# The smaller key by VectorE, the larger by GpSimd: sharing a bitonic sort's compare and exchange

## The reference, cut to what matters

```python
src = jnp.concatenate([edge_index[0], loops])      # 524288 edges, 50176 nodes
dst = jnp.concatenate([edge_index[1], loops])
e = jax.nn.leaky_relu(a_src[src] + a_dst[dst], negative_slope=0.2)
e_max = jax.ops.segment_max(e, dst, num_segments=M)
ee = jnp.exp(e - e_max[dst])
denom = jax.ops.segment_sum(ee, dst, num_segments=M)
```

## Time and profile before

| what | value |
|---|---|
| median of 3 runs | 11034.17 us (11019.4 to 11040.31) |
| the profiled execution's own time | 11027.03 us |
| its span in the trace | 11025.2 us |
| VectorE busy | 5592.9 us, 51% of the span |
| GpSimd busy | 6152.7 us, 56% |
| TensorE busy (products) | 4769.1 us, 43% |
| ScalarE busy | 3867.4 us, 35% |

### The profile page before, as it was taken

How to read it: one execution, slowest core, us unless ns; L and a number is a source line. 1 busy time by engine, 2 the same in 40 slices (tenths; PEclk the granted TensorE clock), 3 DMA queues, 4 the chain that set the end, 5 groups by cost and what they waited for, 6 DMA issues and landing times. The chain is left out here.

```text
span 11025.2 us, 125122 instructions
## 1 busy us (share of the span) xinstructions
PE 4769.1 (43%) x29069; PEld 2965.3 (27%) x29069; DVE 5592.9 (51%) x14901; ACT 3867.4 (35%) x9265; POOL 6152.7 (56%) x6259
## 2 busy tenths in 40 slices
PE   0111777777775998784232232232222323323000
PEld 0111666666663554552011011011111101101000
DVE  9997988888886776552121121211211212112477
ACT  0011777777772555332121121121111212212255
POOL 0000444444441221676777777777777777777675
PEclk9755999998996999887666666666666666666555
DMA  0000111111112222553222222222222222222366
GB/s 21 0 0 36 36 32 35 35 32 35 32 35 78 62 61 59 142 147 74 44 47 49 40 51 45 41 51 43 45 48 45 47 44 45 50 40 48 137 237 240
DMA packets 1325844, 659.79 MB, mean 60 GB/s; under 512 B 1058255, under 2 KB 1239100, under 8 KB 1320764
## 3 DMA queue, kind: packets, MB, share of 16 engines
q1 hardware_dynamic: 1142396, 576.49, 19.2%
q0 software_dynamic: 183104, 80.22, 6.2%
HBM read 344.86 MB, written 313.71 MB: 60 GB/s over the span
## 5 line engine op out<-in xcount | busy, mean ns | idle before, releaser
L1843 POOL DMA_INDIRECT gr_rec<-rec,gr_idx x4096 | 3963.3, 968 | 1248.8 <-issue 1247.9
L1864 PE MATMUL gr_p_h<-gr_tT,gr_w 128*128 128x512 f32 x1568 | 848.0, 695 | 3682.3 <-ACT gr_hT L1898 3648.9
L1983 DVE TENSOR_SCALAR gr_pen<-gr_same 128x64 f32<-128x64 f32 x64 | 13.7, 215 | 3170.5 <-DMA gr_rec<-rec,gr_idx 3170.5
L1864 PEld LDWEIGHTS gr_p_h<-gr_tT,gr_w 128*128 128x128 f32 x1568 | 347.0, 226 | 4164.8 <-ACT gr_hT L1898 3734.0
L549 POOL TENSOR_TENSOR at_sq<-at_qk 128x256 f32<-128x256 f32 x392 | 263.9, 673 | 2121.3 <-ACT at_qk L591 2118.9
L1911 ACT ACTIVATE gr_ee<-gr_dd 128x512 f32<-128x512 f32 x64 | 40.3, 629 | 3598.4 <-DVE gr_dd L2002 3598.4
L1869 PE MATMUL gr_p_y<-gr_hT,gr_w 128*128 128x512 f32 x1568 | 688.9, 592 | 0.0
L1963 DVE STREAM_TRANSPOSE gr_z<-gr_yb 128x2048 f32<-128x2048 f32 x98 | 226.5, 2311 | 895.4 <-ACT gr_yb L1903 863.9
L1898 ACT ACTIVATE gr_hT<-gr_p_h,gr_b 128x512 f32<-128x512 f32 x784 | 517.8, 688 | 190.2 <-PE gr_p_h L1864 186.9
L2151 POOL DMA_INDIRECT cb_a<-scan,cb_idx x392 | 503.9, 1286 | 133.7 <-issue 121.1
L1347 POOL DMA_INDIRECT adst<-co_rec,co_idx x448 | 422.8, 944 | 202.5 <-issue 148.5
(11 more groups left out here) (364 smaller groups left out, 13262.2 us busy)
## 6 DMA issues: line engine op xcount, KB each, us to landing
y<-gr_z SPq DMA_DIRECT2D x392, 256.0 KB, 5.2
cb_y<-y SPq DMA_DIRECT2D x28, 3584.0 KB
gr_rec<-rec,gr_idx POOLq DMA_INDIRECT x4096, 2.4
scan<-gr_out SPq DMA_DIRECT2D x64, 768.0 KB, 3.5
at_xs<-in_x_win SPq DMA_DIRECT2D x56, 448.0 KB, 3.9
x<-at_x SPq DMA_DIRECT2D x56, 448.0 KB, 4.5
ff_x<-x SPq DMA_DIRECT2D x56, 448.0 KB, 3.3
x<-ff_x SPq DMA_DIRECT2D x784, 32.0 KB
```

The costliest lines, as they stand in the source:

```text
L1843: nc.gpsimd.indirect_dma_start(out=rec[s][:, j, :], out_offset=None, in_=rec_dram, in_offset=bass.IndirectOffsetOnAxis(ap=idx[s][:, j:j + ...
L1864: nc.tensor.matmul(p_h[m % 4][:, :], w1[:, P * m:P * (m + 1)], tT[b.k][:, :], start=True, stop=True).then_inc(S["hp"], 1)
```

## The change

In every stage the 2048 pairs of a partition are split: 1280 (five eighths) stay with VectorE alone, and for 768 (three eighths) the minimum is still VectorE's, while GpSimd makes the maximum. It reads both keys as integers and adds them (32 bits) into a new tile `so_both`; when VectorE's minimum is there, it subtracts it from the sum, and what is left is the larger key's bits. One stage then has three VectorE instructions (a minimum of 768 pairs, a minimum and a maximum of 1280 pairs) and two GpSimd instructions (a sum and a difference, 768 elements each).

`pairs` chooses the columns. Up to width 256 GpSimd's pairs are all in columns 2560 to 4095; above that they are the last three eighths of each group. Two successive stages of width 256 or less thus touch the two column ranges independently, and `near` marks the second of such a pair (145 of the 190 stages): there the sum and the first minimum wait only for the last stage's first minimum and last difference. In the other 45 stages both engines wait for all of the stage before. The counter `pooled` counts GpSimd's instructions, and the flips, the turns and the code behind the sort wait for it as well.

```diff
+        both = sb("so_both", [P, EP // 2], I32)
+        pooled = Steps(sem("so_pooled"))
+        OWN = 2560
+        def pairs(tile, d, mirror, pool):
+            if d <= 256:
+                cols = tile[:, OWN:EP] if pool else tile[:, 0:OWN]
+                view = cols.rearrange("p (g h s) -> p g h s", h=2, s=d)
+                return view[:, :, 0, :], view[:, :, 1, ::-1] if mirror and d > 1 else view[:, :, 1, :]
+            lo, hi = (5 * d // 8, d) if pool else (0, 5 * d // 8)
+            view = tile.rearrange("p (g h s) -> p g h s", h=2, s=d)
+            if mirror:
+                return view[:, :, 0, lo:hi], view[:, :, 1, d - 1 - lo:d - 1 - hi if hi < d else None:-1]
+            return view[:, :, 0, lo:hi], view[:, :, 1, lo:hi]
...
-                at.append((s, m, t, f))
+                at.append((s, m, t, f, l))
+                small = item[0] == "stage" and item[3] <= 256
+                near.append(small and last)
+                last = small
                 if item[0] == "stage":
-                    s += 2
+                    s += 3
+                    l += 2
...
+            @block.gpsimd
+            def _(pool):
+                for item, by, (s, m, t, f, l) in zip(plan, near, at):
...
+                    lo, hi = pairs(a[:, :].bitcast(I32), d, mirror, True)
+                    small, large = pairs(b[:, :].bitcast(I32), d, mirror, True)
...
+                    pool.wait_ge(stepped.sem, s - 2 if by else s)
+                    if l:
+                        pool.wait_ge(pooled.sem, l)
+                    if m:
+                        pool.wait_ge(moved.sem, m)
+                    pooled.done_by(nc.gpsimd.tensor_tensor(sums, lo, hi, ALU.add))
+                    pool.wait_ge(pooled.sem, l + 1)
+                    pool.wait_ge(stepped.sem, s + 1)
+                    pooled.done_by(nc.gpsimd.tensor_tensor(large, sums, small, ALU.subtract))
...
-                        v.wait_ge(done.sem, s)
+                        v.wait_ge(done.sem, s - 2 if by else s)
+                        if l:
+                            v.wait_ge(pooled.sem, l)
...
-                        done.done_by(nc.vector.tensor_tensor(bv[:, :, 0, :], av[:, :, 0, :], av[:, :, 1, r], ALU.min))
-                        done.done_by(nc.vector.tensor_tensor(bv[:, :, 1, r], av[:, :, 0, :], av[:, :, 1, r], ALU.max))
+                        lo, hi = pairs(a[:, :], d, mirror, True)
+                        small, _ = pairs(b[:, :], d, mirror, True)
+                        done.done_by(nc.vector.tensor_tensor(small, lo, hi, ALU.min))
+                        lo, hi = pairs(a[:, :], d, mirror, False)
+                        small, large = pairs(b[:, :], d, mirror, False)
+                        if by:
+                            v.wait_ge(done.sem, s)
+                        done.done_by(nc.vector.tensor_tensor(small, lo, hi, ALU.min))
+                        done.done_by(nc.vector.tensor_tensor(large, lo, hi, ALU.max))
```

More of the change, by code:

```diff
@@ L183, in sort_edges @@
         with nc.Block() as block:
-            at, s, m, t, f = [], 7, 0, 0, 0
+            at, s, m, t, f, l = [], 7, 0, 0, 0, 0
+            near, last = [], False
             for item in plan:
-                at.append((s, m, t, f))
+                at.append((s, m, t, f, l))
+                small = item[0] == "stage" and item[3] <= 256
+                near.append(small and last)
+                last = small
                 if item[0] == "stage":
-                    s += 2
+                    s += 3
+                    l += 2
                 elif item[0] == "flip":
@@ L212, in _ @@
                 act.wait_ge(loaded, 64)
-                for item, (s, m, t, f) in zip(plan, at):
+                for item, (s, m, t, f, l) in zip(plan, at):
                     if item[0] == "flip":
@@ L216, in _ @@
                         act.wait_ge(stepped.sem, s)
+                        act.wait_ge(pooled.sem, l)
                         for c in range(NCH):
@@ L235, in _ @@
                     pe.wait_ge(stepped.sem, s)
+                    pe.wait_ge(pooled.sem, l)
                     if m:
@@ L244, in _ @@
                         last.then_inc(turned.sem, 1)
+            @block.gpsimd
+            def _(pool):
+                for item, by, (s, m, t, f, l) in zip(plan, near, at):
+                    if item[0] != "stage":
+                        continue
+                    _, a, b, d, mirror = item
+                    lo, hi = pairs(a[:, :].bitcast(I32), d, mirror, True)
+                    small, large = pairs(b[:, :].bitcast(I32), d, mirror, True)
+                    n = lo.shape[1] * lo.shape[2]
+                    sums = both[:, 0:n].rearrange("p (g s) -> p g s", g=lo.shape[1])
+                    pool.wait_ge(stepped.sem, s - 2 if by else s)
[7 more added lines that the diff above has]
+                    pooled.done_by(nc.gpsimd.tensor_tensor(large, sums, small, ALU.subtract))
             @block.vector
@@ L264, in _ @@
                 done.done_by(nc.vector.tensor_scalar(ka[:, :], kb[:, :], sgn[:, 0:1], None, ALU.mult))
-                for n, (item, (s, m, t, f)) in enumerate(zip(plan, at)):
+                for n, (item, by, (s, m, t, f, l)) in enumerate(zip(plan, near, at)):
                     if n == 8:
@@ L272, in _ @@
                         _, a, b, d, mirror = item
-                        v.wait_ge(done.sem, s)
+                        v.wait_ge(done.sem, s - 2 if by else s)
+                        if l:
+                            v.wait_ge(pooled.sem, l)
                         if m:
                             v.wait_ge(moved.sem, m)
-                        av = a[:, :].rearrange("p (g h s) -> p g h s", h=2, s=d)
-                        bv = b[:, :].rearrange("p (g h s) -> p g h s", h=2, s=d)
-                        r = slice(None, None, -1) if mirror and d > 1 else slice(None)
-                        done.done_by(nc.vector.tensor_tensor(bv[:, :, 0, :], av[:, :, 0, :], av[:, :, 1, r], ALU.min))
-                        done.done_by(nc.vector.tensor_tensor(bv[:, :, 1, r], av[:, :, 0, :], av[:, :, 1, r], ALU.max))
+                        lo, hi = pairs(a[:, :], d, mirror, True)
[7 more added lines that the diff above has]
+                        done.done_by(nc.vector.tensor_tensor(large, lo, hi, ALU.max))
                     elif item[0] == "turn":
@@ L285, in _ @@
                             done.done_by(nc.vector.tensor_copy(b[:, 512 * c:512 * c + 512], banks[c][:, :]))
-                assert done.n == end
+                assert done.n == end and pooled.n == l + 2 * (item[0] == "stage")
                 v.wait_ge(done.sem, end)
+                v.wait_ge(pooled.sem, pooled.n)
                 bits = final[:, :].bitcast(I32)
@@ L301, in _ @@
                 done.done_by(nc.vector.tensor_tensor(other[:, 1:EP], final[:, 1:EP], final[:, 0:EP - 1], ALU.is_equal))
-        clear(nc, (loaded, stepped.sem, scaled.sem, turned.sem, moved.sem, stored, *bias.sem.values()))
+        clear(nc, (loaded, pooled.sem, stepped.sem, scaled.sem, turned.sem, moved.sem, stored, *bias.sem.values()))
 def row_signs():
```

## The result

The changed kernel takes 11500.47 us (median of 4 runs, 11492.13 to 11505.98) against 11037.24 us for the kernel before in the same comparison: ratio 1.0421, 95% interval 1.0405 to 1.0438. That is 463 us more. The forecast was 11,510 us.

A forecast was written before the change was run, and what follows sets the result against it. VectorE was taken to bound the bare sort, 962.8 us. Engines taking turns add 358 us in near stages and 120 us in the others, 478 us onto 11027.0, giving 11,510 us; 8-in-10 range 11,300 to 11,850.

The forecast's parts named there:

- The bound: Sort plan: 962.8 us, VectorE working 896.7 us, GpSimd idle; nothing overlaps the sort, 4.53 us a stage.
- the gift: Sort stages: VectorE's own work falls from 4.53 to 3.81 us, 137 us less over 190 stages.
- The collision: Sort stages: VectorE and GpSimd instructions reading SBUF run one after another; a stage's five do not overlap; 70 in 100.
- The price of GpSimd's instructions: GpSimd's sum and difference in each stage: 1.78 us each for 768 elements, integers priced like float additions.
- The order of the turns: Near stages: 6.9 us if both queues always have something waiting, 7.15 if VectorE keeps its turn; middle 7.0 taken.
- the sum: Whole sort: 145 near stages +358 us, 45 others at 7.2 us +120 us, together +478 us.
- Everything behind it is untouched: The part behind the sort, 10025.7 us, does not change.
- Side by side: Rival, sort stages: both engines overlap, 129 us saved, 10,905 us; chance 8 in 100.
- Quick integers: Rival, GpSimd's integer instructions: 0.83 us each at the copy's rate, 5.1 us a stage, 11,150 us; chance 10 in 100.
- slow ones: Rival, GpSimd's integer instructions: up to twice the float price, about 11,850 or 12,190 us; chance 12 in 100.
- a start-up and a handoff: Stages where both engines wait: 0.14 us of start-up and 0.1 us of handoff come on top.

The follow-up runs named there:

- ScalarE in GpSimd's place: Changed kernel with ScalarE copying the upper key of the 768 pairs instead of GpSimd's work, larger key not made: 10927.54 us, ratio 0.9893 to the kernel before.
- fills: Kernel before plus two GpSimd scratch memsets of 768 integers in each sort stage, nothing waiting for them: 11040.97 us, ratio 1.0006.
- the additions: Kernel before plus two GpSimd scratch additions of 768 integers in each sort stage, nothing in the sort waiting for them: 11604.0 us, ratio 1.0519.
- the copies: Kernel before plus two GpSimd scratch copies of 768 integers in each sort stage: 11245.79 us, ratio 1.0195.
- scratch additions with PSUM: Kernel before plus two GpSimd scratch additions a stage, ScalarE first copying upper keys to PSUM as one VectorE operand: 11471.03 us, ratio 1.0398.
- the version through PSUM: Near stages: ScalarE copies upper keys to PSUM, GpSimd makes 768 larger keys; other stages as before the change: 10974.67 us, ratio 0.9937 to kernel before.

## Why the prediction was right

**The bound and the gift.** The sort is bare and VectorE's, as read from the earlier trace rows. VectorE alone was forecast at 3.81 us a stage; with ScalarE in GpSimd's place a near stage was 3.67 us, since a near stage's first minimum does not wait for the maximum before it, and they overlap by their ends as well. The plan's stretch is 804.1 us there against 962.8, so the gift is 159 us where I had 137. In that run the time fell by 120 us only (11047.76 to 10927.54), because the part behind the sort took 10091.7 us in its profile, the longest of all. Some of that is the longer rest of all kernels of this kind; its keys are also not in order, so the later parts gather other rows, which may be the remainder and was not tested.

**The collision.** This step decided the sign, and it came from a handful of overlapping records in another part of the program. It held for plain minima as for the spread-out operand there, and for instructions two to three times as long. The experiments narrow it: GpSimd must read (fills cost nothing, one operand is enough), and VectorE must have both operands in SBUF (one in PSUM costs nothing), as the earlier trace rows suggested with one pair of records. The Trainium skill, SBUF — State Buffer, section "Who interferes with whom", states just these conditions: a VectorE instruction with two SBUF inputs contends with a GpSimd instruction that reads SBUF, and not with one that only writes it. The runs agree on every one that they touch: 3.77 us in place of 2.29 for the additions, 2.79 for the copies, 2.29 for the fills, and 2.28 with one operand in PSUM.

**The price of GpSimd's instructions.** Forecast 1.78 us free and 1.64 us in turn, taken from float additions; measured 1.81 us free (median in the scratch additions with PSUM) and 1.64 to 1.66 us in turn, so integers cost what was reckoned from floats; only the sums of width 1 and 2 were cheaper.

**The order of the turns.** I left open whether VectorE keeps its turn for two instructions that wait for nothing, and took the middle, 7.0 us. In 189 of the 190 stages GpSimd gets in between L328 and L329. That is the lower bound of the two, 6.87 us against 6.86 from the terms. The other stages are 7.01 us in place of 7.2. It is not a fixed rule, though. In the stage at 94 us, the first behind three small VectorE instructions of the bias table, VectorE kept its turn, and GpSimd's difference was held through both and ended 1.69 us behind L329:

```profile
94.55 1.47 DVE L328 TENSOR_TENSOR so_kb<-so_ka 128x1280 f32<-128x1280 f32 x1
94.76 4.35 POOL L287 TENSOR_TENSOR so_kb<-so_both,so_kb 128x768 int32<-128x768 int32 x1 [3.03 <-DVE so_kb L323]
95.95 1.47 DVE L329 TENSOR_TENSOR so_kb<-so_ka 128x1280 f32<-128x1280 f32 x1
```

Who gets the turn was thus chosen without a row to go by, and what decides it is still open.

**The size.** The near stages' turns are 19 us less than the sum had, the other stages' 9 us, and the cheaper additions below 15 us: together 43 us, which makes 435 us of the 478. "Everything behind it is untouched" was wrong the other way, by 28 us in the medians. That the total came within 10 us of the forecast is in part luck, since the two errors offset each other. The mechanism and the size of the loss in the sort don't rest on that.

**The rivals.** Side by side was wrong here and right as soon as one operand left SBUF. Quick integers were wrong; slow ones too. The waits cost less than the sum had: 0.16 us a stage where they are made stricter, against 0.24 us for a start-up and a handoff.

## What to carry to other kernels

Before work is shared between VectorE and GpSimd, look in the trace for records of the two that overlap and compare each duration with its free one; if the later one ends behind the earlier by its full work, a second engine adds its time and saves only what it took over. Here the operands' place decided it: with one of VectorE's operands in PSUM the same sharing gained. And in a collision busy time misleads; the ends of successive instructions show the work. Last, a part of the program that a change doesn't touch can still grow with it, which shows in the medians of several variants and not in one pair of profiles.

## What the runs showed of the hardware that was not expected

Among the near stages those of width 1 and 2 are quicker than all others: 6.58 us from one first minimum to the next against 6.88 us. VectorE's first minimum in the changed kernel, in a stage of width 1, in one of width 4, and in the one behind it:

```profile
49.94 2.22 DVE L323 TENSOR_TENSOR so_kb<-so_ka 128x768 f32<-128x768 f32 x1
...
56.52 2.56 DVE L323 TENSOR_TENSOR so_ka<-so_kb 128x768 f32<-128x768 f32 x1
...
63.41 2.21 DVE L323 TENSOR_TENSOR so_kb<-so_ka 128x768 f32<-128x768 f32 x1
```

It is GpSimd's sum that is shorter. In the version through PSUM, where nothing collides, the sum ranges from 1.46 us to a median of 1.80 us for the same 768 elements; the short ones are those of width 1 and 2 (the second and third line, a width of 1 and one of 4):

```profile
L297 POOL TENSOR_TENSOR so_both<-so_kb x73: 1464/1801/1828, 41.7 to 925.7; 128x768 int32<-128x768 int32 x73
...
45.83 1.47 POOL L297 TENSOR_TENSOR so_both<-so_ka 128x768 int32<-128x768 int32 x1
...
49.85 1.82 POOL L297 TENSOR_TENSOR so_both<-so_kb 128x768 int32<-128x768 int32 x1
```

Scratch additions of dense rows take 1.81 us, and the difference, with one dense operand, 1.80 to 1.86 us at every width. A sum whose operands lie in single columns or in pairs of columns takes 19% less time than a dense one; from runs of four columns on there is no difference. Why, no run here tells.
